# Attention output stored by features in DRAM and divided by its sums in the output stage; TensorE's order of firsts, weighing, firsts, seconds

## The chip, the core and the metric

One core of a Trainium2 chip runs the whole program as one launch. Its engines (TensorE or PE, VectorE or DVE, ScalarE or ACT, GpSimd or POOL, SyncE or SP, which here only issues DMAs) have instruction queues of their own, run each queue in order, and wait for one another on semaphores. The metric is the device time of one execution in microseconds (us). Before the change the median of 3 runs is 2280.14 us.

## The reference

Four layers on x of 4 x 512 tokens by 512 features, each followed by a layer norm over `x + layer(x)`: a state space scan, routed experts, attention, and a gated layer with quantised input. The change touches attention alone:

```python
q, k, v = (proj(w_q), proj(w_k), proj(w_v))                 # 32 heads of 16 features
scores = jnp.einsum('bhqd,bhkd->bhqk', q, k) / jnp.sqrt(jnp.float32(D_K))
attn = jax.nn.softmax(scores, axis=-1)
out = jnp.einsum('bhqk,bhkd->bhqd', attn, v)
out = out.transpose(0, 2, 1, 3).reshape(B, S, HIDDEN)
return jnp.einsum('bse,oe->bso', out, w_o)
```

## The kernel before

The program is a row of blocks with a barrier between them: the scan's inputs and the scan, a norm, the router and shared experts, the sorted experts, a second norm, `project` (q, k in two parts `hi` and `lo`, and v, all written to DRAM), `attend`, `attention_out`, a third norm, and the gated layer. Nothing of a block starts before the barrier, except for loads that were prefetched: `attend` loads and splits the output weights (`wo_ahead`).

`attend` goes over 32 sets of four heads of one batch entry; a set has 4 steps (`kt` 0 to 3), of 128 keys in the one role and 128 queries in the other, 128 steps in all. The softmax needs the maximum of each query's scores first, so each score is computed twice:

- **first** (`first(step, pair)`, L1396): two matmuls give scores with queries on partitions, one 128 x 512 bank each, out of a ring of three banks (`FIRSTS = 3`). VectorE reduces each bank to its maximum (L1524). Firsts run 8 steps (`LEAD`), two sets, ahead. A pair of firsts waits until the reduces of all but the last bank before it are done.
- **turn_max** (L1410): the set's negated maxima (L1532, L1536 on VectorE) are transposed on TensorE into a bank of the seconds' ring of two, copied by ScalarE to `rows` (L1494), and brought by two DMAs (L1348, `load_max`) into extra rows of `qs`, where the seconds add them.
- **second** (L1418): two matmuls give scores with keys on partitions, minus the maximum; ScalarE takes the exponential of 128 x 1024 elements into `prob` (L1486). The ring of two is shared with `turn_max`: `second_free` waits for whoever read the bank two places earlier.
- **weigh** (L1432): four matmuls multiply the probabilities by v, with a column of ones in v, so that `p_out` has for each head 16 features and the sum, on partitions of features. It runs a step behind.
- **copy_out** (L1497), **turn_out** (L1446), **divide** (L1540): once a set, ScalarE copies `p_out` to `o_sb`, TensorE transposes it in four pieces into a bank of the firsts' ring, and VectorE takes the reciprocals and multiplies into `g.Y`.

SP's queue (L1364 on) issues, per set, two copies of the maxima, twelve loads of `qs` and `ks` and one of `v` for the set four ahead.

`attention_out` (L1577) goes over 16 token tiles. TensorE transposes four 128 x 128 pieces of `g.Y` (L1598), ScalarE and VectorE split them into `th` and `tl`, and 12 matmuls (`three`, L126 to L130, for four chunks of features) multiply by the output weights; VectorE adds `g.X`. The transposes of a tile are issued ahead of the products of the tile before.

`scoped(..., reused=True)` ends a stage with a block in which GpSimd clears the stage's semaphores (L67 to L77), so that their numbers can be used again.

## Time and profile before

| what | us |
|---|---|
| median of 3 runs (2273.37 to 2288.04) | 2280.14 |
| the profiled execution | 2278.79 |
| its span, first to last instruction | 2277.0 |
| busy in the span: PE / DVE / ACT / POOL | 1837.9 / 1630.4 / 814.1 / 734.1 |
| `attend`, first product to last division | 1191.5 to 1634.7 |
| of it at the low clock | until about 1247 |
| `attention_out` | 1635.0 to 1688.3 |

The page gives busy time of the engines, and groups of instructions by line with their count, busy time, mean length and the idle time before them with what ended it. A timeline gives single instructions in order: start, length, engine, line, operation, shapes, count of merged instructions, and in brackets the idle time before it. Matmul records have modelled ends and overlap, so distances between starts are read, not lengths. In attention a record marked x2 is a pair of matmuls on two halves of the rows; the four matmuls of a weighing give 8 records. TensorE's granted clock stands in the busy table by stretch, as a share of 2.4 GHz. For a DMA, the time in SP's queue is the issuing; the landing is when its semaphore has come.

### The profile page before, as it was taken

The page shows a single profiled execution, that of the slowest core. Times are in us where ns is not written, and L with a number is a line of the kernel's source. Part 1 is how long each engine was busy: PE and PEld are TensorE (multiplying, and loading weights), DVE is VectorE, ACT ScalarE, POOL GpSimd, SP SyncE. Part 2 cuts the span into 40 slices and gives each one's busy share as a digit, 9 for nine tenths or more (in the row PEclk, how much of TensorE's full clock was granted, in tenths as well). Part 3 has the DMA queues.
Part 4 walks back from the last instruction along what each step waited for, and adds up shares of the span by engine and source line. Part 5 has one row for each costly group of instructions (what it writes and reads, how often), then busy time and mean ns, then how long its engine had stood idle before and what let it go on. Part 6 is the DMA issues. An engine that isn't in the chain of part 4 may idle for free. (4 is left out here: it accounts for less than half of the span.)

```text
span 2277.0 us, 27810 instructions
## 1 busy us (share of the span) xinstructions
PE 1837.9 (81%) x8232; PEld 1108.7 (49%) x8232; DVE 1630.4 (72%) x2905; ACT 814.1 (36%) x1301; POOL 734.1 (32%) x582
## 2 busy tenths in 40 slices
PE   5287778787658899927977888888873999999998
PEld 1022222222436888815862333333452777777786
DVE  4699999999634657774206888888458776667668
ACT  5243434343211435421213777777623111111112
POOL 2676767674250656663001000000011332113100
PEclk8599999999879879957995999999985999999999
DMA  8011111111030878853543333333000000000002
GB/s 300 23 42 38 37 37 37 37 37 32 12 148 8 275 237 296 277 175 136 193 185 97 93 81 92 85 91 88 5 30 28 28 28 28 1 28 28 1 1 75
DMA packets 102032, 197.64 MB, mean 87 GB/s; under 512 B 17257, under 2 KB 34025, under 8 KB 101019
## 3 DMA queue, kind: packets, MB, share of 16 engines
q1 hardware_dynamic: 96795, 179.46, 24.3%
q0 software_dynamic: 5120, 16.78, 2.3%
q8 instruction: 54, 0.88, 0.2%
q14 instruction: 63, 0.52, 0.1%
HBM read 130.72 MB, written 63.05 MB: 85 GB/s over the span
## 5 line engine op out<-in xcount | busy, mean ns | idle before, releaser
L1524 DVE TENSOR_REDUCE att_top<-att_first 128x1 f32<-128x512 f32 x512 | 332.2, 686 | 123.3 <-PE att_first L1407 116.0
L421 PE MATMUL scan_y<-scan_hc,all_ident 128*128 128x512 f32 x512 | 294.6, 663 | 101.6 <-DVE scan_hc L381 101.5
L355 POOL TENSOR_TENSOR scan_dbx<-ssm_U,scan_bbc 128x512 f32<-128x512 f32 x256 | 316.4, 1270 | 134.5 <-DVE scan_h L390 101.2
L390 DVE TENSOR_TENSOR_SCAN scan_h<-scan_da,scan_dbx 128x512 f32<-128x512 f32 x256 | 309.3, 1209 | 22.8 <-POOL scan_dbx L355 21.9
L1486 ACT ACTIVATE att_prob<-att_second 128x1024 f32<-128x1024 f32 x256 | 257.0, 1020 | 99.6 <-PE att_second L1427 93.4
L366 ACT ACTIVATE scan_da<-ssm_DT,ssm_A 128x512 f32 x256 | 176.7, 691 | 270.7 <-DVE scan_h L390 270.6
L421 PEld LDWEIGHTS scan_y<-scan_hc,all_ident 128*128 128x128 f32 x512 | 79.1, 194 | 313.8 <-DVE scan_hc L381 313.1
L1670 POOL TENSOR_TENSOR pairs_raw<-pairs_raw,pairs_scales 128x512 f32<-128x512 f32 x42 | 42.5, 1048 | 548.2 <-DMA pairs_raw<-in_w 548.2
L1407 PE MATMUL att_first<-att_ks,att_qs 48*128 48x512 f32 x512 | 135.8, 520 | 73.8 <-DVE att_top L1524 62.9
L1800 ACT ACTIVATE ffn_silu<-ffn_pg 128x256 f32<-128x256 f32 x112 | 43.2, 386 | 414.9 <-PE ffn_pg L130 414.8
L128 PE MATMUL ffn_pg<-pairs_wh,last_XH 128*128 128x512 f32 x448 | 180.4, 403 | 1.7 <-PEq L431 1.7
L129 PE MATMUL ffn_pg<-pairs_wl,last_XH 128*128 128x512 f32 x448 | 178.8, 399 | 0.0
L130 PE MATMUL ffn_pg<-pairs_wh,last_XL 128*128 128x512 f32 x448 | 178.2, 398 | 0.0
L381 DVE TENSOR_TENSOR scan_hc<-scan_cbc,scan_h 128x512 f32<-128x512 f32 x256 | 169.1, 662 | 0.0
L1407 PEld LDWEIGHTS att_first<-att_ks,att_qs 48*128 48x128 f32 x512 | 54.4, 194 | 225.4 <-DVE att_top L1524 157.9
L1824 DVE TENSOR_TENSOR ffn_h<-ffn_pg,ffn_silu 128x256 f32<-128x256 f32 x112 | 47.4, 423 | 136.8 <-ACT ffn_silu L1800 136.7
L1442 PE MATMUL att_out<-att_prob,att_v 128*32 128x512 f32 x1024 | 140.7, 622 | 0.9 <-ACT att_prob L1486 0.8
L1427 PE MATMUL att_second<-att_qs,att_ks 56*128 56x512 f32 x512 | 117.3, 446 | 4.4 <-DMA att_qs<-att_rows 3.2
L1677 POOL TENSOR_SCALAR pairs_wh<-pairs_raw 128x512 fp32r<-128x512 f32 x42 | 24.8, 622 | 241.2 <-PE ffn_py L130 241.2
L410 PE MATMUL scan_cbc<-ssm_CT,ssm_sel 16*128 x128 | 72.4, 651 | 36.8 <-DVEq L372 36.8
L128 PE MATMUL ffn_py<-pairs_wh,ffn_hh 128*128 128x512 f32 x224 | 98.3, 439 | 0.0
L130 PEld LDWEIGHTS ffn_pg<-pairs_wh,last_XL 128*128 128x128 f32 x448 | 85.5, 191 | 21.8
(272 smaller groups left out, 3901.1 us busy)
## 6 DMA issues: line engine op xcount, KB each, us to landing
mlps_raw<-in_w SPq DMA_DIRECT2D x26, 769.0 KB, 6.2
exp_raw<-in_w SPq DMA_DIRECT2D x24, 769.0 KB, 5.9
scan_bbc<-brow_dram SPq DMA_DIRECT2D x64, 256.0 KB, 3.2
sorted_x<-pre_zero SPq DMA_DIRECT2D x4, 3072.0 KB, 15.2
exp_x<-sorted_x SPq DMA_DIRECT2D x48, 256.0 KB, 4.4
sorted_y<-exp_y SPq DMA_DIRECT2D x48, 256.0 KB, 4.4
att_qs<-qk_dram SPq DMA_DIRECT2D x192, 64.0 KB, 2.2
att_ks<-qk_dram SPq DMA_DIRECT2D x192, 64.0 KB, 2.2
```

Source lines behind the costliest of these rows:

```text
L128: pe.matmul(out, lh, rh, start=first, stop=False)
L129: pe.matmul(out, lh, rl, start=False, stop=False)
L130: return pe.matmul(out, ll, rh, start=False, stop=last)
L355: nc.gpsimd.tensor_tensor(dbx[:, i % (2 * KC), :], g.U[:, c, bass.ts(b, NB)], bbc[:, n % RING, :], ALU.mult).then_inc(dbx_ready, 1)
L366: nc.scalar.activation(da[:, i % 2, :], g.DT[:, c, bass.ts(b, NB)], ACT.Exp, scale=g.A[:, c, n:n + 1]).then_inc(da_ready, 1)
L381: nc.vector.tensor_tensor(hc[:, i % 2, :], cbc[:, (i // KC) % 2, :], h[:, i % HRING, :], ALU.mult).then_inc(hc_ready, 1)
L390: nc.vector.tensor_tensor_scan(h[:, i % HRING, :], da[:, i % 2, :], dbx[:, i % (2 * KC), :], 0.0, ALU.mult, ALU.add).then_inc(h_ready, 1)
L421: mm = pe.matmul(y[:, c, :], g.ident[:], hc[:, i % 2, :], start=(m == 0), stop=(m == STATE - 1))
L1407: pe.matmul(p_first[first_place(m) % FIRSTS][:], qs[w % RING][at, pair, qt * P:(qt + 1) * P], ks[w % RING][at, pair, :], start=True, stop= ...
L1442: mm = pe.matmul(p_out[VPAD * j:VPAD * (j + 1), :], v[s % RING][:, kt, VPAD * j:VPAD * (j + 1)], prob[step % 2][:, j, :], start=(kt == 0), ...
L1486: nc.scalar.activation(prob[step % 2][:, js, :], p_second[second_place(step, pair) % 2][:], ACT.Exp, scale=DK ** -0.5).then_inc(exp_done, 1)
L1524: nc.vector.tensor_reduce(top[w % 2][:, qt, item:item + 1], p_first[first_place(m) % FIRSTS][:], AX.X, ALU.max).then_inc(max_done, 1)
```

## The change

1. The transposes and the division leave `attend`. `copy_out` stays. SP then issues, per set, eight stores (`store_out`): for each of the four heads the 16 feature rows to `o_dram` and the row of sums to `sum_dram`. They stand behind the loads of their turn of the loop. `o_sb` is free again when they have landed. The ring of three banks holds firsts alone.
2. TensorE's order in a step. Before: second, firsts, second, weighing, firsts, with `turn_max` at the end of step kt = 1. After: firsts, weighing, firsts, and then both seconds of the next step, with `turn_max` at the end of step kt = 0, so behind the seconds of kt = 1 as before, but without the products that stood between.
3. `attention_out` goes over the 4 batch entries. Per batch SP loads the sums (64 KB) and the output by features (1 MB), VectorE inverts the sums, SP stores them to `inv_dram` and reads them back eight times, each spread over 16 partitions (`spread`). VectorE multiplies (4 operations of 128 x 512), ScalarE makes `th`, GpSimd makes `tl`, and TensorE runs the same 12 matmuls per tile with four output banks, without transposes.
4. `ln2` and `wo` now clear their semaphores at their end; a few semaphores that must not be cleared there are made once for the program.

```diff
+        sb, ps, sem = scoped(nc, ctx, tag, reused=by_feature or gather)
         stats = sb("stats", [P, TILES, 6])
...
                              rows[w % 2][:].bitcast(F32).unsqueeze(1).to_broadcast([2 * SET, PAIRS, NB])
                              ).then_inc(m_in[w % RING], 16)
+
+        def store_out(sp, s):
+
+            sp.wait_ge(o_copied, s + 1)
+            b, head = s // (HEADS // SET), s % (HEADS // SET) * SET
+            for j in range(SET):
+                at = j * VPAD
+                feature = (head + j) * DK
+                sp.dma_start(g.o_dram[b, feature:feature + DK, :], o_sb[s % 2][at:at + DK, :]).then_inc(o_stored[s % 2], 16)
+                sp.dma_start(g.sum_dram[b, head + j:head + j + 1, :], o_sb[s % 2][at + DK:at + DK + 1, :]
+                             ).then_inc(o_stored[s % 2], 16)
         @block.sync
...
+                if s:
+                    store_out(sp, s - 1)
+            store_out(sp, SETS - 1)
+            for k in range(2):
+                sp.wait_ge(o_stored[k], 128 * SETS // 2)
         @block.gpsimd
...
-                for k in range(2):
-                    m = 4 * step + 2 * pair + k
-                    first_free(first_place(m))
+                if step or pair:
+
+                    pe.wait_ge(max_done, 4 * step + 2 * pair + 2 - FIRSTS)
                 for k in range(2):
...
-            def turn_out(s):
-
-                pe.wait_ge(o_copied, s + 1)
-                first_free(out_place(s))
-                for qt in range(STEPS):
-                    mm = pe.transpose(p_first[out_place(s) % FIRSTS][:, qt * P:(qt + 1) * P],
-                                      o_sb[s % 2][:, qt * P:(qt + 1) * P], g.ident[:])
-                mm.then_inc(o_turned, 1)
-
             for step in range(LEAD):
                 for pair in range(PAIRS):
                     first(step, pair)
                 if step == STEPS:
                     turn_max(0)
+            second(0, 0)
+            second(0, 1)
             for step in range(TOTAL):
                 s, kt = step // STEPS, step % STEPS
-                second(step, 0)
                 if step + LEAD < TOTAL:
                     first(step + LEAD, 0)
-                second(step, 1)
                 if step:
                     weigh(step - 1)
                 if step + LEAD < TOTAL:
                     first(step + LEAD, 1)
-                if kt == 1 and s + 1 < SETS:
+                if step + 1 < TOTAL:
+                    second(step + 1, 0)
+                    second(step + 1, 1)
+                if kt == 0 and s + 1 < SETS:
                     turn_max(s + 1)
-                if kt == 2 and s:
-                    turn_out(s - 1)
             weigh(TOTAL - 1)
-            turn_out(SETS - 1)
         @block.scalar
...
-                    act.wait_ge(o_turned, s - 1)
+                    act.wait_ge(o_stored[s % 2], 128 * (s // 2))
                 nc.scalar.activation(o_sb[s % 2][:], p_out[:], ACT.Copy).then_inc(o_copied, 1)
...
+        sums = [sb(f"sums{k}", [P, P]) for k in range(2)]
+        o = [sb(f"o{k}", [P, KC, NB]) for k in range(2)]
+        r = [sb(f"r{k}", [P, KC, NB]) for k in range(2)]
+        th = [sb(f"th{k}", [P, KC, NB], F32R) for k in range(2)]
+        tl = [sb(f"tl{k}", [P, KC, NB], F32R) for k in range(2)]
+        po = [ps(f"po{k}", [P, DIM]) for k in range(4)]
+        sums_in, r_in, o_in = [sem("sums_in0"), sem("sums_in1")], [sem("r_in0"), sem("r_in1")], [sem("o_in0"), sem("o_in1")]
+        inverted, r_stored, scaled = sem("inverted"), [sem("r_stored0"), sem("r_stored1")], sem("scaled")
+        hi_ready, lo_ready, product, added = sem("hi_ready"), sem("lo_ready"), sem("product"), sem("added")
         block = ctx.enter_context(nc.Block())
+        PER = HEADS // KC
+        @block.sync
+        def _(sp):
+            def load_sums(b):
+                sp.dma_start(sums[b % 2][:], g.sum_dram[b].rearrange("h (q t) -> (h q) t", t=P)).then_inc(sums_in[b % 2], 16)
+                if b >= 2:
+                    sp.wait_ge(lo_ready, KC * (b - 1))
+                sp.dma_start(o[b % 2][:], g.o_dram[b].rearrange("(c p) t -> p c t", p=P)).then_inc(o_in[b % 2], 16)
+            def spread(b):
+                sp.wait_ge(inverted, b + 1)
+                sp.dma_start(g.inv_dram[b].rearrange("h (q t) -> (h q) t", t=P), sums[b % 2][:]).then_inc(r_stored[b % 2], 16)
+                sp.wait_ge(r_stored[b % 2], 16 * (b // 2 + 1))
+                for k in range(PER):
+                    sp.dma_start(r[b % 2][k * DK:(k + 1) * DK, :, :],
+                                 g.inv_dram[b].rearrange("(c k) t -> k c t", k=PER)[k].partition_broadcast(DK)
+                                 ).then_inc(r_in[b % 2], 16)
+            load_sums(0)
+            load_sums(1)
+            for b in range(BATCH):
+                spread(b)
+                if b + 2 < BATCH:
+                    load_sums(b + 2)
+        @block.gpsimd
+        def _(pool):
+            for b in range(BATCH):
+                for c in range(KC):
+                    n = KC * b + c
+                    pool.wait_ge(hi_ready, n + 1)
+                    if b >= 2:
+                        pool.wait_ge(product, PER_BLOCK * (b - 1))
+                    pool.tensor_tensor(tl[b % 2][:, c, :], o[b % 2][:, c, :], th[b % 2][:, c, :].bitcast(F32),
+                                       ALU.subtract).then_inc(lo_ready, 1)
         @block.tensor
         def _(pe):
+            for t in range(TILES):
+                b, j = t // PER_BLOCK, t % PER_BLOCK
+                if j == 0:
+                    pe.wait_ge(lo_ready, KC * (b + 1))
+                if t >= 4:
+                    pe.wait_ge(added, t - 3)
+                for c in range(KC):
+                    w = slice(c * DIM, (c + 1) * DIM)
+                    cols = slice(j * P, (j + 1) * P)
+                    mm = three(pe, po[t % 4][:], th[b % 2][:, c, cols], tl[b % 2][:, c, cols], wh[:, w], wl[:, w],
+                               c == 0, c == KC - 1)
+                mm.then_inc(product, 1)
         @block.scalar
         def _(act):
+            for b in range(BATCH):
+                for c in range(KC):
+                    n = KC * b + c
+                    act.wait_ge(scaled, n + 1)
+                    if b >= 2:
+                        act.wait_ge(product, PER_BLOCK * (b - 1))
+                    nc.scalar.activation(th[b % 2][:, c, :], o[b % 2][:, c, :], ACT.Copy).then_inc(hi_ready, 1)
         @block.vector
         def _(dve):
+            def invert(b):
+                dve.wait_ge(sums_in[b % 2], 16 * (b // 2 + 1))
+                nc.vector.reciprocal(sums[b % 2][:], sums[b % 2][:]).then_inc(inverted, 1)
+            def scale(b):
+                dve.wait_ge(r_in[b % 2], 16 * PER * (b // 2 + 1))
+                dve.wait_ge(o_in[b % 2], 16 * (b // 2 + 1))
+                for c in range(KC):
+                    nc.vector.tensor_tensor(o[b % 2][:, c, :], o[b % 2][:, c, :], r[b % 2][:, c, :],
+                                            ALU.mult).then_inc(scaled, 1)
+            def add(t):
+                dve.wait_ge(product, t + 1)
+                nc.vector.tensor_tensor(g.Y[:, t, :], po[t % 4][:], g.X[:, t, :], ALU.add).then_inc(added, 1)
+            invert(0)
+            invert(1)
+            scale(0)
+            for b in range(BATCH):
+                if b + 1 < BATCH:
+                    scale(b + 1)
+                if b + 2 < BATCH:
+                    invert(b + 2)
+                for j in range(PER_BLOCK):
+                    add(PER_BLOCK * b + j)
```

The rows below are the instructions in their order on one engine, from the program itself. First TensorE in `attend`, in a set of the steady part. L1407 are the firsts, L1427 the seconds, L1442 the weighing, L1414 `turn_max`, L1451 `turn_out`. Before:

```order
L1414 MATMUL att_second<-all_ident,att_minus 8x128 x4
L1427 MATMUL att_second<-att_qs,att_ks 128x512 x2
L1407 MATMUL att_first<-att_ks,att_qs 128x512 x2
L1427 MATMUL att_second<-att_qs,att_ks 128x512 x2
L1442 MATMUL att_out<-att_prob,att_v 32x512 x4
L1407 MATMUL att_first<-att_ks,att_qs 128x512 x2
L1451 MATMUL att_first<-all_ident,att_o_sb 128x128 x4
L1427 MATMUL att_second<-att_qs,att_ks 128x512 x2
L1407 MATMUL att_first<-att_ks,att_qs 128x512 x2
L1427 MATMUL att_second<-att_qs,att_ks 128x512 x2
L1442 MATMUL att_out<-att_prob,att_v 32x512 x4
```

After, where L1400 are the firsts, L1420 the seconds, L1435 the weighing and L1407 `turn_max`:

```order
L1400 MATMUL att_first<-att_ks,att_qs 128x512 x2
L1420 MATMUL att_second<-att_qs,att_ks 128x512 x4
L1407 MATMUL att_second<-all_ident,att_minus 8x128 x4
L1400 MATMUL att_first<-att_ks,att_qs 128x512 x2
L1435 MATMUL att_out<-att_prob,att_v 32x512 x4
L1400 MATMUL att_first<-att_ks,att_qs 128x512 x2
L1420 MATMUL att_second<-att_qs,att_ks 128x512 x4
L1400 MATMUL att_first<-att_ks,att_qs 128x512 x2
L1435 MATMUL att_out<-att_prob,att_v 32x512 x4
```

Between the two pairs of firsts of a step only the weighing is left, the four matmuls of two seconds follow each other, and the transposes of the maxima directly follow the second pair whose bank's neighbour they take; `turn_out` is gone.

SP's queue in the output stage after the change (the stage had no DMAs before). L1563 and L1567 are `load_sums`, L1571 and L1574 `spread`:

```order
L1563 DMA wo_sums<-sum_dram 128x128
L1567 DMA wo_o<-o_dram 128x4x512
L1563 DMA wo_sums<-sum_dram 128x128
L1567 DMA wo_o<-o_dram 128x4x512
L1571 DMA inv_dram<-wo_sums 128x128
L1574 DMA wo_r<-inv_dram 16x4x512 x8
L1563 DMA wo_sums<-sum_dram 128x128
L1567 DMA wo_o<-o_dram 128x4x512
L1571 DMA inv_dram<-wo_sums 128x128
L1574 DMA wo_r<-inv_dram 16x4x512 x8
```

The third load of `o_dram` reuses the first batch's tile and so waits for the first batch's subtractions; the second batch's `spread` stands behind it.

## Rows read from the trace of the kernel before

**Rows 1.** The page, costliest groups: two VectorE operations.
```profile
L1524 DVE TENSOR_REDUCE att_top<-att_first 128x1 f32<-128x512 f32 x512 | 332.2, 686 | 123.3 <-PE att_first L1407 116.0
...
L381 DVE TENSOR_TENSOR scan_hc<-scan_cbc,scan_h 128x512 f32<-128x512 f32 x256 | 169.1, 662 | 0.0
```

**Rows 2.** Busy time by stretch: attention at full clock; the output stage.
```profile
1250.00:1600.00 350.00, 302.94 (x1966) 110.42 (x1966) 301.62 (x546) 249.10 (x272) 0.00 (x0) 1.00 0.33 87
1635.00:1688.30 53.30, 51.59 (x256) 42.27 (x256) 22.01 (x32) 9.48 (x16) 0.00 (x0) 1.00 0.00 1
```

**Rows 3.** Timeline, one attention step and a half: start us, length us, engine, line.
```profile
1420.45 0.40 PE L1427 MATMUL att_second<-att_qs,att_ks 56*128 56x512 f32 x2
...
1420.92 1.03 ACT L1486 ACTIVATE att_prob<-att_second 128x1024 f32<-128x1024 f32 x1 [0.67 <-PE att_second L1427]
...
1424.52 0.50 PE L1407 MATMUL att_first<-att_ks,att_qs 48*128 48x512 f32 x2 [0.64 <-DVE att_top L1524]
...
1425.18 1.06 PE L1442 MATMUL att_out<-att_prob,att_v 128*32 128x512 f32 x8
...
1426.18 0.49 PE L1407 MATMUL att_first<-att_ks,att_qs 48*128 48x512 f32 x2
...
1426.61 0.60 PE L1414 MATMUL att_second<-all_ident,att_minus 128*8 128x128 f32 x4
1426.71 2.62 DVE L1524 TENSOR_REDUCE att_top<-att_first 128x1 f32<-128x512 f32 x4 [0.40 <-PE att_first L1407]
...
1427.14 0.50 PE L1427 MATMUL att_second<-att_qs,att_ks 56*128 56x512 f32 x2
...
1427.55 0.51 PE L1407 MATMUL att_first<-att_ks,att_qs 48*128 48x512 f32 x2
```

**Rows 4.** Timeline of the DMA queue (SP), one set of four heads.
```profile
1427.86 1.45 SPq L1348 DMA_DIRECT2D att_qs<-att_rows  x2
1429.35 2.77 SPq L1337 DMA_DIRECT2D att_qs<-qk_dram  x6
...
1434.96 0.43 SPq L1340 DMA_DIRECT2D att_v<-v_dram  x1
1440.70 1.45 SPq L1348 DMA_DIRECT2D att_qs<-att_rows  x2
```

**Rows 5.** One line's DMA issues: ns minimum/median/maximum, a 16 x 512 store to DRAM.
```profile
L187 SPq DMA_DIRECT2D brow_dram<-pre_brow x4: 332/333/347, 17.0 to 45.8; - x4
```

**Rows 6.** DMA issues over the whole span: count, KB each, median us to landing.
```profile
qk_dram<-proj_hi SPq DMA_DIRECT2D x32, 256.0 KB, 2.0
...
att_v<-v_dram SPq DMA_DIRECT2D x32, 256.0 KB, 2.9
...
ssm_D<-in_dcoef SPq DMA_DIRECT2D x1, 2.0 KB, 5.0
```

**Rows 7.** View of L1174: two loads of 1 MB issued one after the other.
```profile
DMA to landing us min/median/max: 5.6/6.9/8.2
```

**Rows 8.** Groups by line: the same subtraction on GpSimd in two stages.
```profile
L1681 POOL TENSOR_TENSOR pairs_wl<-pairs_raw,pairs_wh 128x512 fp32r<-128x512 f32 x42 | 52.8, 1297 | 0.0
...
L1041 POOL TENSOR_TENSOR mlps_wl<-mlps_raw,mlps_wh 128x512 fp32r<-128x512 f32 x24 | 47.2, 1968 | 15.4 <-ACT mlps_wh L1104 15.2
```

**Rows 9.** Timeline of TensorE as the projections start after idle time.
```profile
1048.26 0.63 PE L130 MATMUL proj_po<-later_XH,wq_lo 128*128 128x512 f32 x1
1048.69 0.63 PE L128 MATMUL proj_po<-later_XH,wq_hi 128*128 128x512 f32 x1
...
1052.52 0.39 PE L128 MATMUL proj_po<-later_XH,wq_hi 128*128 128x512 f32 x1
1052.75 0.40 PE L129 MATMUL proj_po<-later_XL,wq_hi 128*128 128x512 f32 x1
```

**Rows 10.** Timeline, from attention's last output copy to the output stage.
```profile
1632.65 0.60 ACT L1502 ACTIVATE att_o_sb<-att_out 128x512 f32<-128x512 f32 x1 [1.19 <-PE att_out L1442]
...
1635.03 1.07 PE L1598 MATMUL wo_pt<-all_ident,all_sums 128*128 128x128 f32 x8 [1.07 <-PEq L1259]
```

87 lines of the change are left out of this document (11 added, 76 removed).

## Prediction, made before the changed kernel ran

> **What bounds the kernel now.** I read the busy time by stretch first, to find the two stretches that the change touches. At full clock attention keeps VectorE busy 301.62 of 350 us, TensorE 302.94 by modelled ends, ScalarE 249.10 [rows 2]. The page's groups then say what the rest of VectorE's time is: the 512 reduces of 0.686 us were preceded by 123.3 us of idle time, 116.0 of it until a first product was there [rows 1]. So neither engine bounds attention alone; the loop between them does, and the timeline shows it. A pair of firsts starts at 1424.52, the weighing at 1425.18, the next pair at 1426.18, the reduce of its first bank at 1426.71 (after 0.40 us of idle time), and a further pair at 1427.55, released by that reduce [rows 3]. Call the pairs A (pair 0 of a step) and B. With three banks, A of a step waits for the reduce of B's first bank in the step before. The loop is A, second, weighing (0.66 after A), B (1.00 later), reduce (0.53), its length 0.69, release (1427.55 less 1426.71 and 0.69: 0.15): 3.03 us. Three of four steps are that; the fourth has VectorE's division and a full turn besides. SP's queue shows the period of a set: its two `att_rows` copies start at 1427.86 and at 1440.70, 12.84 us, of which issuing took 7.53 (to 1434.96 + 0.43) [rows 4]. The output stage is TensorE's: 16 tiles in 53.3 us, busy 51.59 of it, GpSimd idle and no DMA moving [rows 2].
>
> **The attention loop, step by step.** Removed per set are 4 transposes, a reciprocal and a multiplication, so the long fourth step goes. The second no longer stands between A and the weighing. Two pairs back to back with the weighing took 0.66, so A to the weighing directly costs from 0.33 (half of it) to 0.43 (a pair followed by transposes over all rows, 1426.18 to 1426.61 [rows 3]). I take 0.41, near the second, since the weighing also uses all rows. An ordinary step becomes 0.41 + 1.00 + 0.53 + 0.69 + 0.15 = 2.78 us. The seconds behind B start at 1.41 + 0.33 = 1.74 and 2.07 and are done before A's release at 2.78; they cost nothing there.
>
> One step in four is different. `turn_max(s + 1)` now stands at kt = 0, right behind the seconds of kt = 1, and its bank is the one that `second(4s + 1, 0)` has just filled, so it waits for that exponential. This is the wait that the change adds, and the next A stands behind it on TensorE. The exponential starts 0.47 after its second (1420.45 to 1420.92) and lasts 1.03 [rows 3]: 1.74 + 0.47 + 1.03 = 3.24, with the release 3.30; the transposes hold TensorE 0.53 (1426.61 to 1427.14): A at 3.83 instead of 2.78. A set is 3.83 + 3 x 2.78 = 12.17, against 12.84: 0.67 less. 30 of 32 sets carry firsts, and about 1.5 of them run at the low clock at the start, which leaves 28.5: **-19.1 us**. With 0.33 the set is 11.85 (-28); with 0.43 it is 12.25 (-17). At the low clock the same wait costs what the shorter loop gives: I take **+0.5**. The last two sets are bound by 16 exponentials in both kernels: 0.
>
> **SP in attention.** Eight stores a set come behind the loads. A 16 x 512 store took 0.332 us to issue [rows 5], the strided loads 2.77 / 6 = 0.46 with their gaps [rows 4]; so 8 x (0.38 to 0.46) = 3.0 to 3.7, and SP works 10.6 to 11.2 of 12.17 us. The maxima's copy waits behind them no longer than it has time: cost 0, cover 1 to 1.6 us per set. Its price if the cover goes is the second rival.
>
> **The hand-over.** Before, the last copy of the output starts at 1632.65 and the output stage's first product at 1635.03, 2.4 us [rows 10]. Now: copy 0.60, eight issues 3.3, landing 2.0 (a store to DRAM [rows 6]), barrier 0.2: 6.1. **+3.7**. The two extra clears of semaphores, each a range clear and a barrier, are taken at 0.4 each; one counts here, **+0.4**, and one below.
>
> **The output stage.** Nothing of it can start ahead, since all loads stand behind the barrier. I count from SP's first issue.
> - Sums, 1 MB of output, sums, 1 MB of output go out by 1.8. The inverted sums' store is issued at 2.7, when the small first load has come (2.2) and the reciprocal is done. Does it queue behind the 2 MB? A 2 KB load issued behind a 1 MB one landed after 5.0, where a store of 256 KB alone took 2.0 [rows 6]. Of two 1 MB loads the second, issued 0.45 after the first, landed after 8.2 [rows 7]; here 9.0. So the store lands at about 9.3 (4.7 if nothing queues).
> - Eight loads of the inverted sums, 0.47 each, the last landing 2.9 after its issue (as 256 KB of `att_v` [rows 6]): 15.4.
> - VectorE's multiplication 0.66 per chunk (as L381 [rows 1]), ScalarE's copy 0.6 and its release, then GpSimd's four subtractions of 1.26 (52.8 / 42 [rows 8]): 15.4 + 0.7 + 0.7 + 5.1 = 21.9. TensorE can start then.
> - The next batch is not ahead. `load_sums(2)` waits for the four subtractions and stands before `spread(1)` in SP's order, as the rows of the order show. So at 22.0 the third 1 MB goes out, the second inverted store behind it (5.8 to land, 5.6 for the megabyte [rows 7]), its eight loads (6.2), the multiplication, copy and subtractions (6.5): a hop of 18.6 us. Batch 1 is ready at 40.5, batch 2 at 59.1.
> - A batch's products, 48 x 0.2275 us at full clock (1052.52 to 1052.75 [rows 9]), take 10.9. Batch 0 ends by 35.3, batch 1 by 53.8; TensorE waits both times. Batch 2 runs from 59.1. Batch 3's store has nothing in front of it and is ready at about 70.3, in time.
> - After waits like these the products begin at the low clock: the projections ran at 0.43 us each (1048.26 to 1048.69) until 1052.5, 5 us from their start at 1047.3 [rows 9]. In batches 0 and 1 this is hidden by the hops; from 59.1 it costs 2.4. End: 59.1 + 21.8 + 2.4 + 0.9 for the last addition + 0.5 for the clear = 84.7.
>
> Against 53.3 [rows 2] that is **+31.4 us**, though 64 transposes are gone (16 x 12 products alone are 43.7).
>
> **A port that two engines share.** The same subtraction took 1.97 us in the experts' stage, where VectorE works on tiles of the SBUF at the same time [rows 8]. At 1.97 a batch is ready 2.8 later, three times: +8.4 at most. The Trainium skill, "SBUF — State Buffer", Who interferes with whom, says that a VectorE operation with two SBUF inputs and a GpSimd operation that reads SBUF lock each other out for a whole instruction; this case's 1.97 beside 1.26 agrees with it. By that rule GpSimd would start when the four multiplications end, 1.3 us later per batch, and the sum would be 3.9 higher. The multiplications take 2.6 of the 6.5 us, so I stay at 1.26 and keep the upper bound for the range.
>
> **Sum.** -19.1 + 0.5 + 3.7 + 0.4 + 31.4 = +16.9 us. The profiled execution took 2278.79 (span 2277.0); it becomes 2295.7. The median of the runs shown is 2280.14, 1.35 higher, so 2297.
>
> **The rivals.**
> - *Nothing queues behind the megabytes.* Then the first inverted store lands at 4.7, the 3 MB move at 3.05 us each by [rows 7] (8.6 less 5.6), batch 0 is ready 4.4 earlier and each hop is 3.0 shorter: 10.4 less, 2287. The 5.0 of the 2 KB load speaks against it.
> - *SP becomes the bound in attention* (slower). The 8-row copies from SBUF are issued at 0.72 each, 1.45 for two [rows 4]. If stores from 16 rows and 1 row cost that, SP needs 7.53 + 8 x 0.75 = 13.5 per set, above 12.84: +19 instead of -19, 2335. The point is (12.84 - 7.53) / 8 = 0.66 per issue. The 0.332 of the same shape speaks against it [rows 5]; the 1-row store has no row. The Trainium skill, "DMA: Bandwidth & Descriptors", Rules for kernel authors, says that transfers under 64 KB pay mostly overhead; these are 32 KB and 2 KB. No row here shows this overhead coming into the time while the queue has room.
> - *The wait of the maxima's turn hides* (faster). Were TensorE free at 2.07 + 0.33 + 0.53 = 2.93, a set would be 11.27: -45, 2271. For this the exponential would have to end 0.9 earlier than its second allows; only records misplaced in time would do that.
> - *The chain of the output stage is heavier*: GpSimd at 1.97, or the low clock costs twice. 2305 to 2312.
>
> **How the numbers follow.** Forecast (2288 to 2304) 0.50; heavier chain 0.20; nothing queues 0.12; SP bound 0.10; hidden wait 0.08. A measurement of this kernel can tell about 1%, 22.8 us, from no change. Slower by more (above 2303) takes SP's case, most of the heavier chain and the forecast's upper edge: 0.33. Faster by more (below 2257) needs the hidden wait and the absent queueing together: 0.05. Within 1%: 0.62. The range leaves out SP's case and the far end of the faster ones: 2278 to 2313.
>
> **What would show it.** In attention: an `att_rows` period of 12.2 us; an idle wait of TensorE for the exponential ahead of the maxima's transposes in every set, none in other steps; SP with 1 us or more of waiting per set. In the output stage: first product 22 us after the stage's first DMA, two waits of 5 us on `lo_ready` 18.6 us apart, clock at 0.5 at times. The prediction is wrong if the period is at or above 12.84, if the store of the inverse lands within 3 us, or if the output stage lies outside 75 to 95 us.

## The result, and the profile of the changed kernel

The changed kernel takes 2302.53 us (median of 4 runs, 2296.81 to 2307.33) against 2280.75 (4 runs, 2273.37 to 2288.04) of the kernel before, run beside it: a ratio of 1.0119, 95% interval 1.0084 to 1.0155. The medians differ by 21.8 us, just under 1%, and the ratio is a little higher. So it is slower, by about as much as a measurement of this kernel can tell from nothing (1%). The profiled execution took 2298.92 us, its span is 2297.1. Against the span of before, 2277.0, it divides so:

| stretch (us) | before | after | difference | predicted |
|---|---|---|---|---|
| up to attention's first product | 1191.5 | 1189.1 | -2.4 | 0 |
| attention, first product to the last weighing's end | 441.1 | 415.3 | -25.8 | -18.6 |
| hand-over, to the output stage's first work | 2.4 | 4.7 | +2.3 | +4.1 |
| output stage, to its last addition | 53.3 | 102.0 | +48.7 | +31.4 with a clear |
| all that follows | 588.7 | 585.9 | -2.8 | 0 |
| sum | | | +20.0 | +16.9 |

The first and the last line hold nothing that was changed but the clears. Both vary from one execution to the next: in the profiled runs below, the projections, which stand ahead of all that the experiments edit, start anywhere between 1030.6 and 1066.8 us. So below I compare stretches of attention and of the output stage, and ratios of kernels timed together, never one span with another.

The groups by line of the changed kernel (line, engine, operation, tiles, count, then busy us and mean ns of one, then idle time before them and what ended it):

```profile
L1508 DVE TENSOR_REDUCE att_top<-att_first 128x1 f32<-128x512 f32 x512 | 331.9, 687 | 116.8 <-PE att_first L1400 100.8
...
L1407 PE MATMUL att_second<-all_ident,att_minus 128*8 128x128 f32 x128 | 19.9, 279 | 30.9 <-ACT att_prob L1470 30.9
...
L1633 DVE TENSOR_TENSOR wo_o<-wo_o,wo_r 128x512 f32<-128x512 f32 x16 | 14.3, 958 | 58.6 <-DMA wo_r<-inv_dram 58.6
```

The first row answers to [rows 1]: the reduces are as long as before and still wait, 116.8 us in all, 100.8 of them for first products. The second is the wait that the change adds: the transposes of the maxima stand 30.9 us for an exponential. The third names the output stage's trouble: VectorE waited 58.6 us, in four waits, for the loads that spread the inverse.

The timeline of the changed kernel's attention around the start of a set (start us, length us, engine, line); it answers to [rows 3]:

```profile
1427.22 0.50 PE L1400 MATMUL att_first<-att_ks,att_qs 48*128 48x512 f32 x2 [0.41 <-DVE att_top L1508]
...
1427.66 1.07 PE L1435 MATMUL att_out<-att_prob,att_v 128*32 128x512 f32 x8
...
1430.63 0.60 PE L1407 MATMUL att_second<-all_ident,att_minus 128*8 128x128 f32 x4 [1.00 <-ACT att_prob L1470]
...
1431.16 0.50 PE L1400 MATMUL att_first<-att_ks,att_qs 48*128 48x512 f32 x2
...
1431.88 1.45 SPq L1331 DMA_DIRECT2D att_qs<-att_rows  x2
...
1433.87 0.50 PE L1400 MATMUL att_first<-att_ks,att_qs 48*128 48x512 f32 x2 [0.32 <-DVE att_top L1508]
...
1436.57 0.50 PE L1400 MATMUL att_first<-att_ks,att_qs 48*128 48x512 f32 x2 [0.30 <-DVE att_top L1508]
```

From one pair A to the next: 3.94 us (1427.22 to 1431.16) with the turn's wait of 1.00 in it, then 2.71 and 2.70; the fourth step is 2.80. A set is 12.14 us, the mean over 18 sets at full clock, against 12.83 before.

TensorE's clock at attention's start, busy time by stretch (stretch, its length, busy us and count of PE, PEld, DVE, ACT, POOL, then granted clock, DMA share, GB/s). Of the kernel before:

```profile
1191.40:1246.40 55.00, 37.64 (x128) 13.03 (x128) 35.26 (x60) 15.12 (x16) 6.43 (x2) 0.50 0.40 108
1247.00:1257.00 10.00, 8.91 (x58) 3.27 (x56) 8.56 (x17) 7.09 (x8) 0.00 (x0) 1.00 0.36 96
```

Of the changed kernel, with the output stage, which answers to [rows 2]:

```profile
1189.10:1226.90 37.80, 21.47 (x66) 8.34 (x68) 25.00 (x43) 6.33 (x7) 5.62 (x2) 0.50 0.49 131
1227.10:1237.00 9.90, 8.09 (x58) 2.91 (x54) 8.72 (x16) 8.21 (x9) 0.62 (x1) 1.00 0.34 99
...
1609.19:1635.68 26.49, 0.00 (x0) 0.00 (x0) 5.47 (x6) 2.46 (x4) 5.70 (x4) 0.50 0.59 129
1635.68:1711.90 76.22, 51.49 (x192) 40.65 (x192) 22.29 (x30) 7.41 (x12) 17.19 (x12) 0.84 0.41 73
```

Attention ran 55 us at the lower level (1.2 GHz) before and 38 us now; in the output stage TensorE does nothing for 26.5 us and then has a mean clock of 0.84. Before it was the stage's bound at 1.00 [rows 2].

The timeline of the changed kernel from the last weighing to the second batch's products; its first row answers to [rows 10]:

```profile
1604.53 0.60 ACT L1486 ACTIVATE att_o_sb<-att_out 128x512 f32<-128x512 f32 x1 [1.19 <-PE att_out L1435]
1605.15 0.30 SPq L1342 DMA_DIRECT2D o_dram<-att_o_sb  x1
1605.50 0.28 SPq L1343 DMA_DIRECT2D sum_dram<-att_o_sb  x1
...
1609.19 0.35 SPq L1563 DMA_DIRECT2D wo_sums<-sum_dram  x1
...
1610.91 0.95 DVE L1627 RECIPROCAL wo_sums<-wo_sums 128x128 f32<-128x128 f32 x1 [25.00 <-DMA wo_sums<-sum_dram]
1611.89 0.33 SPq L1571 DMA_DIRECT2D inv_dram<-wo_sums  x1
...
1618.29 3.61 SPq L1574 DMA_DIRECT2D wo_r<-inv_dram  x8
...
1628.50 3.57 DVE L1633 TENSOR_TENSOR wo_o<-wo_o,wo_r 128x512 f32<-128x512 f32 x4 [12.14 <-DMA wo_r<-inv_dram]
...
1629.93 5.70 POOL L1594 TENSOR_TENSOR wo_tl<-wo_o,wo_th 128x512 fp32r<-128x512 f32 x4 [402.21 <-ACT wo_th L1621]
...
1635.66 0.38 SPq L1567 DMA_DIRECT2D wo_o<-o_dram  x1
...
1635.68 0.80 PE L128 MATMUL wo_po<-wo_ahead_hi,wo_th 128*128 128x512 f32 x1 [31.22 <-POOL wo_tl L1594]
...
1636.08 0.50 SPq L1571 DMA_DIRECT2D inv_dram<-wo_sums  x1
...
1641.54 3.60 SPq L1574 DMA_DIRECT2D wo_r<-inv_dram  x8
...
1651.44 3.57 DVE L1633 TENSOR_TENSOR wo_o<-wo_o,wo_r 128x512 f32<-128x512 f32 x4 [19.37 <-DMA wo_r<-inv_dram]
...
1658.61 0.38 SPq L1567 DMA_DIRECT2D wo_o<-o_dram  x1
```

The store of the inverse goes out at 1611.89 and SP goes on at 1618.29, so it landed only after 6.4 us. The eight loads that follow are all there at 1628.50, 10.2 us after the first was issued. Products start at 1635.68. The second batch's store is issued behind the third batch's output, at 1636.08, and the second batch's products start at 1658.6 (the load at 1658.61 waits for the same signal): a hop of 23.0 us. The third and fourth start at 1683.1 and 1699.3.

### The profile page after: what moved, and what is told of

The parts are those of the page before. It is cut to its first block and busy times, and to the rows that moved or that the text cites. A ratio compares the mean times of both kernels' runs of the same rounds, so it can differ in the third digit from the quotient of the medians.

```text
span 2297.1 us, 27417 instructions
## 1 busy us (share of the span) xinstructions
PE 1796.1 (78%) x8040; PEld 1087.0 (47%) x8040; DVE 1613.7 (70%) x2845; ACT 804.5 (35%) x1301; POOL 756.5 (33%) x598
## 5 line engine op out<-in xcount | busy, mean ns | idle before, releaser
L1508 DVE TENSOR_REDUCE att_top<-att_first 128x1 f32<-128x512 f32 x512 | 331.9, 687 | 116.8 <-PE att_first L1400 100.8
L421 PE MATMUL scan_y<-scan_hc,all_ident 128*128 128x512 f32 x512 | 294.3, 662 | 102.0 <-DVE scan_hc L381 102.0
L390 DVE TENSOR_TENSOR_SCAN scan_h<-scan_da,scan_dbx 128x512 f32<-128x512 f32 x256 | 317.0, 1239 | 22.9 <-POOL scan_dbx L355 22.1
L1470 ACT ACTIVATE att_prob<-att_second 128x1024 f32<-128x1024 f32 x256 | 248.0, 1022 | 110.0 <-PE att_second L1420 108.0
L381 DVE TENSOR_TENSOR scan_hc<-scan_cbc,scan_h 128x512 f32<-128x512 f32 x256 | 177.0, 693 | 0.0
L1400 PE MATMUL att_first<-att_ks,att_qs 48*128 48x512 f32 x512 | 133.8, 518 | 53.0 <-DVE att_top L1508 41.9
L1594 POOL TENSOR_TENSOR wo_tl<-wo_o,wo_th 128x512 fp32r<-128x512 f32 x16 | 22.9, 1462 | 448.6 <-ACT wo_th L1621 448.6
L1400 PEld LDWEIGHTS att_first<-att_ks,att_qs 48*128 48x128 f32 x512 | 50.6, 191 | 207.4 <-DVE att_top L1508 164.1
L1435 PE MATMUL att_out<-att_prob,att_v 128*32 128x512 f32 x1024 | 138.3, 613 | 0.7 <-ACT att_prob L1470 0.7
L128 PEld LDWEIGHTS ffn_pg<-pairs_wh,last_XH 128*128 128x128 f32 x448 | 84.9, 189 | 22.4 <-issue 2.0
```

The source lines that it names most:

```text
L128: pe.matmul(out, lh, rh, start=first, stop=False)
L381: nc.vector.tensor_tensor(hc[:, i % 2, :], cbc[:, (i // KC) % 2, :], h[:, i % HRING, :], ALU.mult).then_inc(hc_ready, 1)
L390: nc.vector.tensor_tensor_scan(h[:, i % HRING, :], da[:, i % 2, :], dbx[:, i % (2 * KC), :], 0.0, ALU.mult, ALU.add).then_inc(h_ready, 1)
L421: mm = pe.matmul(y[:, c, :], g.ident[:], hc[:, i % 2, :], start=(m == 0), stop=(m == STATE - 1))
L1400: pe.matmul(p_first[m % FIRSTS][:], qs[w % RING][at, pair, qt * P:(qt + 1) * P], ks[w % RING][at, pair, :], start=True, stop=True).then_in ...
L1435: mm = pe.matmul(p_out[VPAD * j:VPAD * (j + 1), :], v[s % RING][:, kt, VPAD * j:VPAD * (j + 1)], prob[step % 2][:, j, :], start=(kt == 0), ...
```

## The experiments

All kernels are edits of the changed kernel unless the text says otherwise. "Stage" is the time from the end of the last weighing to the last addition of the output stage: 55.7 us before, 106.7 after. "A set" is the mean period of a set of four heads over 18 sets at full clock. Kernels named in one paragraph as timed together share their runs of the kernel before.

### Is attention shorter through the order, or through what left it?

The first kernel has the output's new way and the old order of TensorE; the second has the new order alone, in the kernel before. The edit of the first:

```diff
-            second(0, 0)
-            second(0, 1)
...
+                second(step, 0)
                 if step + LEAD < TOTAL:
                     first(step + LEAD, 0)
+                second(step, 1)
                 if step:
                     weigh(step - 1)
                 if step + LEAD < TOTAL:
                     first(step + LEAD, 1)
-                if step + 1 < TOTAL:
-                    second(step + 1, 0)
-                    second(step + 1, 1)
-                if kt == 0 and s + 1 < SETS:
+                if kt == 1 and s + 1 < SETS:
                     turn_max(s + 1)
```

> The changed kernel with TensorE's order in attention put back: second, firsts, second, weighing, firsts in each step, and the turn of the next set's maxima after step 1 instead of step 0; output through DRAM as changed. Theory (the order matters only through the turn's wait): with the turn after step 1 no step waits 1 us for the exponentials of a weighing just issued, so a set takes 12.0 to 12.4 us against 12.14 and the kernel 2295 to 2310 us, ratio to the changed kernel's 2302.5 within 0.5%. Rival (the order is what shortened the loop): a step costs some 0.3 us more, a set 13.3, 32 sets 37 us more, the kernel about 2335.

> The kernel before with the new order of TensorE alone (firsts, weighing, firsts, the next step's seconds, the turn of the maxima after step 0); the output is turned and divided inside attention and the output stage is the old one. Theory (the shorter attention comes from the turn and the divide that left, the order adds nothing while it puts the turn's wait on the path): a set stays at 12.7 to 13.0 us, the kernel at 2275 to 2290, ratio to before 0.998 to 1.004. Rival (the order brought the gain of attention, 0.7 us a set): a set of 12.1, the kernel at 2258, ratio 0.990.

Timed together: the old order with the new way out takes 2305.5 us, ratio to before 1.0117 (1.0048 to 1.0186), the changed kernel's own 1.0119. The order alone takes 2276.2, ratio 0.9995 (0.9963 to 1.0028). A set is 12.06 us in the first and 12.92 in the second; attention as a whole 412.2 and 439.9 us, where the kernels before and after have 441.1 and 415.3. So in both kernels the theory held: taking the transposes and the division away is worth 28.9 us of attention, the order alone 1.2, and on top of the removal it costs 3.1. These totals also hold the start at the low clock, which was as long as 55 us only in the one profile of the kernel before. By the sets at full clock the removal is worth 0.77 us a set, and the new order costs 0.09 alone and 0.08 on top of it. The maxima's transposes (the view of their line: idle time before them, times) say why. In the first kernel:

```profile
L1407 PE MATMUL att_second<-all_ident,att_minus x128: 272/273/417, 1208.9 to 1591.7; 128*8 128x128 f32 x128
its engine sat idle before it (us, times) until:
  issue: 8.3, 31
```

In the second:

```profile
L1414 PE MATMUL att_second<-all_ident,att_minus x128: 269/271/417, 1224.0 to 1632.7; 128*8 128x128 f32 x128
its engine sat idle before it (us, times) until:
...
  ACT att_prob L1489: 30.8, 31
```

With the old order they never wait for an exponential; with the new one 31 of the 32 turns wait 1.0 us each.

### Is that wait on the path?

```diff
+                if kt == 1 and s + 1 < SETS:
+                    turn_max(s + 1)
                 if step:
                     weigh(step - 1)
...
-                if kt == 0 and s + 1 < SETS:
-                    turn_max(s + 1)
```

> The changed kernel with one move: the turn of the next set's maxima (L1407) is issued in step 1, between its first pair of firsts and its weighing, instead of at the end of step 0; the maxima of the next set are then waited for where TensorE would wait for exponentials anyway. Theory (the 1.00 us wait of L1407 for the exponential is on the path): the wait falls away or to under 0.3, the dear step goes from 3.93 to about 3.4, a set from 12.14 to 11.6 to 11.8, the kernel from 2302.5 to 2287 to 2293. Rival (the wait is cover for ScalarE, which then comes late elsewhere): a set stays at 12.1, the kernel within 3 us of 2302.5.

2294.61 us, ratio to before 1.0076 (1.0033 to 1.0118), timed with the two above. The turns wait 6.5 us in all instead of 30.9:

```profile
L1407 PE MATMUL att_second<-all_ident,att_minus x128: 269/271/421, 1226.6 to 1599.2; 128*8 128x128 f32 x128
its engine sat idle before it (us, times) until:
  issue: 15.7, 31
  ACT att_prob L1470: 6.5, 30
```

A set is 11.71 us; attention takes 402.7, 12.6 less than in the changed kernel. The rival is out: every step of the set but this one keeps its 2.70 to 2.80, and the dear one falls from 3.94 to 3.50. By the medians the whole kernel gained 7.9 us and missed the 2287 to 2293 of the theory by little. Its 10 runs lie between 2285.9 and 2319.46, and the interval of its ratio overlaps that of the changed kernel, so the gain rests on the trace of attention and not on the kernels' times.

The same move in the kernel before, with the new order and the old output stage:

> The kernel before with the new order of TensorE and the turn of the maxima moved into step 1 as in e3_turn_late; the output is turned and divided in attention as before and the old output stage stays. Theory (the turn's wait stands on the path in this kernel too): a set goes from the 12.92 us of e2_order_only to 12.4 to 12.6, attention is 10 to 16 us shorter than in e2_order_only, and the ratio to before is 0.993 to 0.996. Rival (with the turn of the output in step 2 ScalarE or VectorE fills the place of that wait): a set stays over 12.8 and the ratio is 0.998 to 1.002.

2250.08 us where before takes 2258.93 in the same runs, ratio 0.9947 (0.9919 to 0.9975). A set is 12.49 us, attention 423.5, 16.4 less than with the order alone; the output stage is untouched at 55.7. The turns now wait 1.0 us in all. So the new order with the turn moved is worth something: 0.34 us a set against the kernel before. The late turn in the old order was not tried.

### What sets the hops of the output stage?

First SP's order. The spreading of batch 1 goes ahead of the load of batch 2, which has to wait for batch 0's split:

```diff
-            for b in range(BATCH):
+            spread(0)
+            spread(1)
+            for b in range(2, BATCH):
+                load_sums(b)
                 spread(b)
-                if b + 2 < BATCH:
-                    load_sums(b + 2)
```

> The changed kernel with another order of SyncE's loads in the output stage only: loads of batches 0 and 1, then the store of the inverse and the eight spreading loads of batch 0, those of batch 1, and only then the sums and output of batch 2 and its spreading, then batch 3. Before, the spreading of batch 1 stood behind the load of batch 2's output, which waits until batch 0 is split. Theory (that wait sets the hops of 23 to 24 us between batches): the second batch's products start 8 to 14 us earlier than the 49.4 us after the stage's start, later hops stay near 24, the kernel goes to 2288 to 2296. Rival (the eight narrow loads themselves set the hop): the second batch starts under 4 us earlier, the kernel stays within 4 us of 2302.5.

2286.74 us, ratio 1.0026 (0.9989 to 1.0064), timed with the first three; the stage takes 87.8 us instead of 106.7, and these 18.9 us are about the kernel's gain (15.8 by the medians, a little more than the 2288 to 2296 of the theory allowed). SP's timeline in this kernel:

```profile
1629.36 3.61 SPq L1574 DMA_DIRECT2D wo_r<-inv_dram  x8
1633.02 0.42 SPq L1571 DMA_DIRECT2D inv_dram<-wo_sums  x1
1639.65 3.58 SPq L1574 DMA_DIRECT2D wo_r<-inv_dram  x8
...
1646.65 0.38 SPq L1567 DMA_DIRECT2D wo_o<-o_dram  x1
```

The second batch's loads now go out at 1639.65, before the wait that ends at 1646.65, not 5.9 us behind it. Its products start 13.7 us after the first batch's instead of 23.0, so 9.2 us earlier. I had expected later hops near 24; they were 12.8 and 16.2. For the two batches that come behind, the store of the inverse landed 1.5 us after its issue, where in the changed kernel the second and third took over 5, and the products of one batch cover what the next one needs.

Then the eight loads. One kernel replaces them by a single one of the same 1 MB over all 128 partitions, another keeps them eight and narrow, but has them read 16 rows each instead of one row 16 times:

```diff
-                for k in range(PER):
-                    sp.dma_start(r[b % 2][k * DK:(k + 1) * DK, :, :],
-                                 g.inv_dram[b].rearrange("(c k) t -> k c t", k=PER)[k].partition_broadcast(DK)
-                                 ).then_inc(r_in[b % 2], 16)
+                sp.dma_start(r[b % 2][:], g.o_dram[b].rearrange("(c p) t -> p c t", p=P)).then_inc(r_in[b % 2], 16)
...
```

> The changed kernel with the eight loads that spread the inverse (16 partitions x 2048 numbers each, 128 KB) replaced by one load of 128 partitions, 1 MB, from the output's own place in DRAM. What is multiplied in is therefore not the inverse of the sums: that part of the computation is changed, all instructions and sizes behind it are as they were. Theory (loads that fill only 16 partitions each come in at about 128 KB in 1.02 us, 10.2 us for eight of them, and a whole one would not): the one load lands 5.5 to 7 us after its issue, and since SyncE issues seven instructions less, each hop between batches falls from 23 to 24.4 us to 17 to 20, and the output stage from 106.7 us behind the last weighing to 85 to 93. Rival (1 MB takes 10 us here whatever its shape): the one load lands after 9 us or more, hops stay over 22.

> The changed kernel with the eight spreading loads kept in number, size and target (16 partitions each), but read from 16 different rows of the output's place in DRAM instead of one row of each block read 16 times; what is multiplied in is not the inverse of the sums, that part is changed. Theory (the narrow target sets the time): the last of the eight lands 9.5 to 10.5 us after the first was issued, as in the changed kernel, and the stage stays at 104 to 109 us. Rival (reading one row 16 times from the same place in DRAM sets it): the last lands 5.5 to 7.5 us after the first issue, the stage ends 8 to 14 us earlier.

Both kernels leave out the division by the sums: they multiply by other numbers of the same size. Each has one execution, so only their traces are read here. The timeline of the kernel with one wide load:

```profile
1607.00 0.36 SPq L1573 DMA_DIRECT2D wo_r<-o_dram  x1
1612.60 3.57 DVE L1630 TENSOR_TENSOR wo_o<-wo_o,wo_r 128x512 f32<-128x512 f32 x4 [7.63 <-DMA wo_r<-o_dram]
```

And of the kernel with eight narrow loads of distinct rows:

```profile
1613.77 3.61 SPq L1574 DMA_DIRECT2D wo_r<-o_dram  x8
1623.23 3.57 DVE L1633 TENSOR_TENSOR wo_o<-wo_o,wo_r 128x512 f32<-128x512 f32 x4 [11.38 <-DMA wo_r<-o_dram]
```

The wide load is there 5.6 us after its issue, the eight narrow ones 9.5 us after the first one's, the changed kernel's 10.2. So eight narrow loads in place of a wide one cost 3.9 us of the difference and the repeated reading 0.7. The two kernels differ in the number of loads as well as in their width, and eight small loads over all 128 partitions were not run. But issuing the eight is over after 3.6 us, and the DMA engines are not idle behind it. The busy table of the middle of each transfer, the eight narrow loads first, then the wide one:

```profile
1616.00:1622.00 6.00, 0.00 (x0) 0.00 (x0) 0.00 (x0) 0.00 (x0) 0.00 (x0) 0.50 1.09 136
...
1609.50:1611.50 2.00, 0.00 (x0) 0.00 (x0) 0.00 (x0) 0.00 (x0) 0.00 (x0) 0.50 1.05 406
```

The DMA share is full in both, at 136 GB/s and at 406, with the same packets of 2 KB; one of them takes 246 ns in the median with the narrow loads and 84 with the wide one. So it is the transfer itself that is slower, and not the issuing. The first two hops are 18.2 and 19.4 us with the wide load and 22.7 and 23.7 with the narrow ones; the stage takes 89.8 and 104.0 us, both in the range of the theory (the second at its edge). 1 MB in 9.5 to 10.2 us is 103 to 110 GB/s. The Trainium skill, "SBUF — State Buffer", Door 1: The DMA port swizzle, says that a transfer into 16 partitions reaches only 4 of the 16 ports, with an asymptote of about 109 GB/s. This case's trace agrees in size: the 1 MB comes in at that rate if the landing is counted in, and at 126 (one row read 16 times) to 136 GB/s in the middle of the transfer. The page's figure is for one transfer, and these are eight to different partitions.

### Without the trip through DRAM

In attention GpSimd writes a matrix of ones and zeros, and in the output stage TensorE spreads the inverse with it. The turn stands late, as above. TensorE's part of the edit:

```diff
...
+            def spread(b):
+                pe.wait_ge(inverted, b + 1)
+                for c in range(KC):
+                    if b:
+                        pe.wait_ge(scaled, KC * (b - 1) + c + 1)
+                    for q in range(PER_BLOCK):
+                        mm = pe.matmul(r[c][:, q * P:(q + 1) * P], g.heads[:, q, c * P:(c + 1) * P], sums[b % 2][:],
+                                       start=True, stop=True)
+                    mm.then_inc(r_ready, 1)
+
+            spread(0)
             for t in range(TILES):
                 b, j = t // PER_BLOCK, t % PER_BLOCK
                 if j == 0:
                     pe.wait_ge(lo_ready, KC * (b + 1))
+                    if b + 1 < BATCH:
+                        spread(b + 1)
...
```

> The turn of the maxima moved as in e3_turn_late, and in the output stage the inverse no longer goes through DRAM: a matrix of ones and zeros, written by GpSimd in attention, spreads it over the 16 features of each head on TensorE (16 matmuls of 128 columns a batch into four PSUM tiles, issued ahead of the products of the batch before), and VectorE multiplies from PSUM. Theory (the trip through DRAM and the eight loads are what makes the stage 106.7 us): the first products start 16 to 19 us behind the last weighing instead of 31, the hops are TensorE's own work, 12.8 + 16 x 0.2 to 0.28 = 16 to 17.3, the stage ends 79 to 84 us behind the last weighing; with a set at 11.7 the kernel takes 2262 to 2274, ratio to before 0.992 to 0.997. Rival (the hop is set by the chain of multiplication, copy and subtraction through GpSimd, not by the loads): hops stay over 20, the stage over 95, the kernel over 2280.

2243.22 us against 2261.73 of before in the same runs, ratio 0.9908 (0.9872 to 0.9945): the first kernel with the output's new way that is faster than the kernel before, and by more than the 0.992 to 0.997 of the theory. The stage takes 75.2 us, under the 79 to 84 forecast, and its hops 14.5 under the 16 to 17.3: from its first products on TensorE has work throughout and keeps its full clock, so a batch's products take 10.9 us (not the 12.8 that I had taken) and the spreading 3.6:

```profile
1608.29:1660.00 51.71, 50.97 (x259) 43.09 (x257) 19.07 (x28) 6.33 (x10) 13.80 (x11) 1.00 0.06 22
```

But the first products start 23.5 us behind the last weighing, where I had forecast 16 to 19. The spreading of batch 1 stood between the ready batch 0 and its products. Two further kernels take the start apart: one loads batch 0 already in attention, the other also issues batch 1's spreading ahead of the wait.

```diff
                 if j == 0:
-                    pe.wait_ge(lo_ready, KC * (b + 1))
                     if b + 1 < BATCH:
                         spread(b + 1)
+                    pe.wait_ge(lo_ready, KC * (b + 1))
```

> As e7_spread_by_matmul, with the loads of the first batch's sums and output issued in attention, after the twelfth set, into tiles of their own. Theory (the stage's start is the landing of that 1 MB, 5.6 us, ahead of multiplication and split): its first products start 3 to 6 us earlier than in e7_spread_by_matmul, later batches too, a set stays at 11.7, and the kernel is 3 to 6 us faster, 2257 to 2270. Rival (the start is bound by GpSimd's four subtractions and the reciprocal, or SyncE in attention has no room for two more DMAs and a wait): less than 2 us.

> As e8_first_batch_ahead, with the spreading matmuls of the second batch placed ahead of TensorE's wait for the first batch's split instead of behind it. Theory (in e8_first_batch_ahead they stood between the ready first batch and its products for 5.0 us, at the low clock in part): the first products start 15 to 16.5 us behind the last weighing instead of 20.2, the stage ends 66 to 69 us behind it instead of 71.9, ratio to before 0.986 to 0.991. Rival (the later batches are bound by the second batch's load and split, which gain nothing): first products earlier, but the stage's end within 1.5 us of 71.9.

The load ahead brings the first products to 20.2 us and the stage to 71.9, both 3.3 less, as forecast. In the kernel's time this does not show: 2242.27 us, ratio 0.9917 (0.9886 to 0.9949), timed with the kernel without it, cannot be told from 0.9908. With both edits the products start 14.5 us behind the last weighing, the stage takes 66.2, and the kernel 2230.91 us against 2258.93, ratio 0.9853 (0.9792 to 0.9914). That is 1.5% faster than the kernel before, by an interval from 0.9 to 2.1%. The timeline of this kernel around its start:

```profile
1582.79 5.28 PE L1603 MATMUL wo_r<-spread_sums_first,spread_heads 128*128 128x128 f32 x32 [5.76 <-DVE spread_sums_first L1641]
...
1586.40 5.08 POOL L1592 TENSOR_TENSOR wo_tl<-spread_o_first,wo_th 128x512 fp32r<-128x512 f32 x4 [371.86 <-ACT wo_th L1632]
...
1587.90 3.74 PE L1603 MATMUL wo_r<-wo_sums,spread_heads 128*128 128x128 f32 x32
...
1591.54 0.50 PE L128 MATMUL wo_po<-wo_ahead_hi,wo_th 128*128 128x512 f32 x1
```

The second spreading (1587.90) now runs while GpSimd splits batch 0, and the products begin as it ends.

## Why the prediction was right, and where its sizes were off

It said 2297 us, slower by 17; it was 2302.5, slower by 22, inside the range. By the medians that is just within the 1% that I had given 0.62, by the ratio just beyond it. That the sum came so near is in part luck. Two of its terms were off by more than the sum shows, 7 us too little gain in attention and 17 too little loss in the output stage, and they cancel in part; the hand-over (2 too much) and stretches that hold nothing of the change (5 shorter) took off the rest. By one of its own signs the prediction was wrong: it called itself so if the output stage lay outside 75 to 95 us, and the stage took 102.0 on the same count, from SP's first issue. The other two signs did not come: the period is 12.14, and the store did not land within 3 us. Of the rivals the heavier chain came nearest, but by neither of the causes that it named: the loads made it heavy, not GpSimd at 1.97 or the low clock.

**Attention, right in mechanism.** An ordinary step was to be 2.78 us and is 2.70 to 2.80; the step with the turn 3.83 and is 3.94; a set 12.17 and is 12.14. The wait was foreseen at its place and in each set, and the kernel with the late turn shows it on the path. SP has room, as foreseen: its stores are issued in 0.30 and 0.28 us, so eight take 2.6 us with their gaps. The term that was mis-sized is the start at low clock. I had put it at +0.5. In fact the first two periods of a set, from one start of the maxima's copies to the next, were 12.42 and 18.87 us and are 9.83 and 13.61: 7.9 us shorter, where two at full clock gain 1.4. The last two sets, which I had put at nothing, gave 1.9 back. The full clock came 38 us after attention's first product instead of 55. It came after 41 to 42 with each of the two halves of the change alone, and after 35 to 42 in every other kernel here. In the four kernels that share the attention with the late turn it varies from 37 to 42, so part of it can be the execution and not the kernel. The kernel before has one profile, and whether its 55 is typical of it stays open, as does what in TensorE's work brings the full clock forward.

**The hand-over** was put at +3.7 and a clear of 0.4; it is +2.3. The stores go out every 0.33 us rather than 0.41, which is 0.7 us; and from the last issue to the stage's first one it took 1.4 us, where I had 2.6 for landing, barrier and clear.

**The output stage, right in its chain, too short in three links.** From SP's first issue (1609.19):
- The inverse's store was to land at 9.3, queued behind 2 MB: 9.1. The rival in which nothing queues is out; it landed 6.4 us after its issue, and in the next two batches 5.4 and 6.7, each behind a megabyte, but 1.5 in the fourth with nothing in front.
- The eight loads were to take 6.1 us, by the landing of `att_v` [rows 6]. They took 10.2. This is the step that failed: `att_v` fills 128 partitions, and these fill 16 each. The row was of a size near enough and of the wrong shape. Each batch pays it, 4 us.
- Multiplication, copy and split were to take 6.5 and took 7.2. Multiplications and subtractions get in each other's way. The view of both lines in the changed kernel (count, then minimum, median and maximum in ns), and of the multiplications in the kernel that spreads by matmul:

```profile
L1633 DVE TENSOR_TENSOR wo_o<-wo_o,wo_r x16: 684/691/1786, 1628.5 to 1693.8; 128x512 f32<-128x512 f32 x16
...
L1594 POOL TENSOR_TENSOR wo_tl<-wo_o,wo_th x16: 1262/1429/1742, 1629.9 to 1698.0; 128x512 fp32r<-128x512 f32 x16
...
L1639 DVE TENSOR_TENSOR wo_o<-wo_o,wo_r x16: 629/689/690, 1596.9 to 1637.5; 128x512 f32<-128x512 f32 x16
```

  In every batch three multiplications take 0.69 us, near the 0.66 of L381 [rows 1], and the fourth 1.76 to 1.79. Of the subtractions the first takes 1.6, the second 1.7 and the last two the 1.26 of [rows 8]. Single records show them taking turns by whole instructions. The first subtraction stands from 1629.93 to 1631.52, and the third multiplication ends at 1630.39; the fourth multiplication stands from 1630.31 to 1632.06, which is 0.69 with what came before it taken for waiting; the second subtraction ends at 1633.19, 1.26 us after 1631.93. So the lock that I had weighed is there, and the step of its sum that was wrong is that GpSimd would start behind all four multiplications, 1.3 us later per batch and 3.9 in all. It gets in behind the third, and a batch pays 0.33 + 0.45 = 0.8 us. With the factor in the PSUM no multiplication takes over 0.69 us and no subtraction over 1.31, though they overlap in time; no run changed the factor's place alone. The upper bound of 1.97 was the mean of two sorts. In the kernel before, 47 of the 48 subtractions of L1041 overlap one of VectorE's (L1135), also from the SBUF, and in all 47 pairs the one that starts second takes over 2.2 us and the first 1.2 to 1.3.
- The reciprocal takes 0.95 us; I had allowed 0.5, but the sums came 0.5 earlier, and the store was issued at 2.7 as forecast.

Ready times were to be 21.9, 40.5, 59.1 and 70.3; they are 26.5, 49.4, 73.9 and 90.1. TensorE's two waits of 5 us became two of 10 and 11 and a third of 3, since batch 3, which was to be in time, is not. The hop through SP's order, which I had read from the rows of the order, is confirmed by the kernel that changes it alone: 19 us of the stage. I had named it and priced it, and had not seen that it could be had back by moving two lines. The cost of the low clock after the waits was put at 2.4 once, and it came to nothing: the products of the first three batches took 12.8, 13.3 and 13.0 us where full clock gives 10.8, but TensorE waited behind each of them, and the fourth ran at full clock.

So the change won more in attention than I had forecast, 26 us instead of 19, and the output stage, with nothing of it hidden and the second and third batch ready 23 to 24 us after the one before, gave back 49 instead of 31.

## What to carry to other kernels

Work that is moved out of a loop whose engines wait for each other is worth its time there; where it goes, count the chain from the first load on, because a stage that was bound by one engine's throughput becomes one bound by latency. Price a DMA by a row of the same shape, and above all of the same number of partitions, before one of the same size. A queue that issues in order should never hold the load that must wait ahead of the one that need not, and a broadcast across partitions inside the chip (here 16 short matmuls, 32 in the trace, 3.6 us) beats a store and eight loads (15 us and more).

## What the runs showed of the hardware

- Eight loads of 128 KB, each into 16 partitions, came in at 9.5 us (distinct rows) and 10.2 us (one row read 16 times) for 1 MB, one load into 128 partitions in 5.6. The DMA engines were busy throughout in the middle of either, at 136 GB/s with the narrow loads of distinct rows and 406 with the wide one.
- A store from the SBUF to DRAM of 16 x 512 is issued in 0.30 us and one of a single row in 0.28, where an 8-row copy within the SBUF needs 0.72 (1.45 for two, in the changed kernel as in [rows 4]).
- A store of 64 KB behind 2 MB of loads lands after 6.4 us, and with nothing ahead of it after 1.5 (the fourth batch's, 1680.31 to 1681.86).
- VectorE's multiplication of 128 x 512 with both inputs in the SBUF took 0.69 us, and 1.76 to 1.79 where it was issued during a subtraction of GpSimd from the SBUF; the subtraction took 1.26, and 1.6 or 1.7 where it was issued during a multiplication. The records fit turns by whole instructions. In the kernel before, in 47 of 47 pairs of subtractions of the two engines from the SBUF, the one that started second took over 2.2 us and the first 1.2 to 1.3. With one input in the PSUM the multiplication took at most 0.69 and the subtraction at most 1.31, overlapping.
- TensorE's granted clock rose to full 55 us after attention's first product in the one profile of the kernel before and after 35 to 42 us in the eleven others; what brings it forward is open.
